# Causal attention stage: output product in two float32r parts with streamed Wo, maxima gathered by ScalarE, cosine product kept in PSUM

## The reference

```python
q = (xn @ Wq).reshape(b, n, h, dh).transpose(0, 2, 1, 3)      # 16 heads of 128
kv = xn @ Wkv
k, v = (kv[..., :dh], kv[..., dh:])                            # one key and value for all heads
q = q * cos + _rotate_half(q) * sin
k = k * cos + _rotate_half(k) * sin
q = q * scale
sim = jnp.einsum('bhid,bjd->bhij', q, k)
sim = jnp.where(causal, neg, sim)
sim = sim - jax.lax.stop_gradient(jnp.max(sim, axis=-1, keepdims=True))
attn = jax.nn.softmax(sim, axis=-1)
out = jnp.einsum('bhij,bjd->bhid', attn, v)
out = out.transpose(0, 2, 1, 3).reshape(b, n, h * dh)
return out @ Wo
```

## Time and profile before

| | us |
|---|---|
| median of 3 runs | 1264.64 (1263.53 to 1266.14) |
| profiled execution | 1257.16 |
| its span, first to last instruction | 1255.4 |
| mean granted TensorE clock in it | 0.949 of 2.4 GHz |
| attention stage in it | from 0 to about 628 |
| an ordinary step of it | 8.62 |
| a group of 8 steps | 74.5 |

### The profile page before, as it was taken

One profiled execution on the slowest core, in us unless ns is written; L12 is line 12 of the kernel. 1 busy time (PEld: TensorE's weight loads), 2 busy tenths in 40 slices (PEclk: granted clock), 3 DMA queues, 4 the chain that ended last, 5 costly groups with the idle time before them and its releaser, 6 DMA issues. The chain is left out here.

```text
span 1255.4 us, 24966 instructions
## 1 busy us (share of the span) xinstructions
PE 1071.3 (85%) x9348; PEld 728.1 (58%) x9348; DVE 889.3 (71%) x1727; ACT 565.6 (45%) x928; POOL 529.9 (42%) x464
## 2 busy tenths in 40 slices
PE   5799999999999999999855789898989963777775
PEld 5577677776777677676422566565666631333332
DVE  7977777777777777768633566767666644888884
ACT  5443333333333333335421466666656542455553
POOL 3644434343343433433324224343434344566653
PEclk9899999999999999999975899999999985899998
DMA  9220000000000000002206666667665310000000
GB/s 351 99 68 25 1 1 1 1 1 0 0 0 0 1 0 0 0 0 70 92 27 147 156 153 170 150 163 164 164 150 128 74 27 32 18 17 25 25 26 26
DMA packets 41903, 80.19 MB, mean 64 GB/s; under 512 B 9424, under 2 KB 23248, under 8 KB 38736
## 3 DMA queue, kind: packets, MB, share of 16 engines
q1 hardware_dynamic: 41136, 78.54, 23.1%
q10 hardware_dynamic: 672, 0.40, 0.1%
HBM read 61.74 MB, written 16.78 MB: 63 GB/s over the span
## 5 line engine op out<-in xcount | busy, mean ns | idle before, releaser
L356 PE MATMUL Yb<-a_Wo,a_oN 128*128 128x512 f32 x512 | 230.8, 594 | 0.0
L1210 DVE TENSOR_REDUCE mx<-Sm 128x4 f32<-128x768 f32 x128 | 122.4, 956 | 89.8 <-PE Sm L950 89.2
L543 POOL TENSOR_TENSOR a_ql<-a_rot,a_qh 128x512 fp32r<-128x512 f32 x64 | 83.9, 1315 | 176.3 <-ACT a_qh L440 176.3
L1048 ACT ACTIVATE x_ex<-Se 128x768 f32<-128x768 f32 x128 | 103.1, 805 | 119.2 <-PE Se L950 119.1
L356 PEld LDWEIGHTS Yb<-a_Wo,a_oN 128*128 128x128 f32 x512 | 97.0, 191 | 98.2 <-issue 92.9
L432 ACT ACTIVATE Lb<-Lb 128x512 f32<-128x512 f32 x64 | 37.2, 582 | 255.7 <-PE Ob L346 255.7
L277 PE MATMUL Qb<-a_xTh,WqH 128*128 128x256 f32 x512 | 146.8, 287 | 4.0 <-DVE a_vl L721 4.0
L278 PE MATMUL Qb<-a_xTl,WqH 128*128 128x256 f32 x512 | 145.5, 284 | 0.0
L279 PE MATMUL Qb<-a_xTh,WqL 128*128 128x256 f32 x512 | 145.4, 284 | 0.0
L557 POOL TENSOR_TENSOR a_pr<-a_pr_plain,a_ph 128x512 fp32r<-128x512 f32 x64 | 83.4, 1304 | 115.6 <-ACT a_ph L427 115.6
L277 PEld LDWEIGHTS Qb<-a_xTh,WqH 128*128 128x128 f32 x512 | 98.7, 193 | 8.0 <-DVE a_vl L721 3.8
(11 more groups left out here) (192 smaller groups left out, 2507.4 us busy)
## 6 DMA issues: line engine op xcount, KB each, us to landing
K<-k_parts SPq DMA_DIRECT2D x32, 256.0 KB, 4.7
q_parts<-x_qp SPq DMA_DIRECT2D x16, 384.0 KB, 3.0
Q<-q_parts SPq DMA_DIRECT2D x16, 384.0 KB, 5.7
k_parts<-x_kp SPq DMA_DIRECT2D x16, 384.0 KB, 7.3
a_w_stage<-in_gateT SPq DMA_DIRECT2D x8, 704.0 KB, 4.1
x_w_stage<-in_gateT SPq DMA_DIRECT2D x8, 704.0 KB, 5.0
WqL_plain<-in_Wq SPq DMA_DIRECT2D x4, 1024.0 KB, 11.4
a_Wo<-in_Wo SPq DMA_DIRECT2D x4, 1024.0 KB, 14.9
```

The source lines that it names most:

```text
L356: mm = pe.matmul(Yb[s % 2][:, :], oN[:, s % 2, i * P:(i + 1) * P], Wo[:, HG * u + i, :], start=(i == 0), stop=(i == HG - 1))
L543: pool.tensor_tensor(rot_dst(False, True, par, r), rbuf(par, r)[:, 0:rot_width(r)], rot_dst(True, False, par, r).bitcast(F32), ALU.subtrac ...
L1048: act.activation(ex[:, (PAIRS * b + p) % RING, 4 * hf * WIN:4 * (hf + 1) * WIN].rearrange("p (j c) -> p j c", j=2), Se[:, :, 0:2 * WIN], A ...
L1210: dve.tensor_reduce(mx[:, half, at:at + 4].rearrange("p (j a) -> p j a", j=2), Sm[:, :, 0:2 * WIN].rearrange("p j (a c) -> p j a c", a=2), ...
```

## The change

The output product is made from float32r parts: ScalarE writes the high part oH of the normalised output, GpSimd the low part oL, and out_projection runs twelve matmuls instead of four float32 ones. Wo gets a high and a low part; both for all heads don't fit in SBUF, so there are two slots, each for a quarter u. In group 0 ScalarE (out_weights_high) and GpSimd (out_weights_low, four instructions of 128 × 512 for each quarter) make them, SyncE stores each pair to DRAM (keep, 2 MB) and loads the third and fourth quarter when the slot has been read; from group 1 on GpSimd issues two 1 MB loads for a slot at the start of each even step (out_weights_again).

The maxima's four copies on VectorE become three on ScalarE, behind the exponentials (maxima_gathered); VectorE joins them after add_to_x (maxima_joined). The rotation makes the sine products first, then the cosine product in place in the PSUM bank, and the sum reads that bank; the banks are freed by rot_ready. The values' high part now waits for rot_ready too. The diff, cut to these parts:

```diff
--- before.py
+++ after.py
...
-        oN = sb("oN", [P, 2, 512], F32)
+        oN, oL = two("oN", [P, 2, 512])
+        oH = sb("oH", [P, 2, 512], F32R)
...
-        Wo = sb("Wo", [P, H, D], F32)
+        WoH = [sb(f"WoH{i}", [P, HG, D], F32R) for i in range(2)]
+        WoLp, WoL = zip(*(two(f"WoL{i}", [P, HG, D]) for i in range(2)))
+        wo_parts = nc.dram_tensor("wo_parts", (U, 2, P, HG * D), F32, kind="Internal").ap()
...
-                    pe.wait_ge(q_free, free(g, USES, j))
+                    if not isinstance(g, int) or g > 0:
+                        pe.wait_ge(rot_ready, done(g - 1, ROTS, ROTS - NG + j))
...
+                if m == 1:
+                    pe.wait_ge(q_free, done(g, NG + 1, NG))
+                elif m > 1:
+                    pe.wait_ge(rot_ready, done(g, ROTS, m - 1))
...
-                pe.wait_ge(oN_ready, done(g, STEPS, s, ON0))
-                if isinstance(g, int) and g == 0 and s % NG == 0:
-                    pe.wait_ge(wo_in[u], 16)
+                pe.wait_ge(oL_ready, done(g, STEPS, s))
+                if isinstance(g, int) and g == 0:
+                    pe.wait_ge(wo_low, HG * (u + 1))
+                else:
+                    pe.wait_ge(wo_in[u % 2], (g - 1) * (32 * U // 2) + 32 * (u // 2 + 1))
 
                 pe.wait_ge(x_new, free(g, STEPS, s))
                 for i in range(HG):
-                    mm = pe.matmul(Yb[s % 2][:, :], oN[:, s % 2, i * P:(i + 1) * P], Wo[:, HG * u + i, :],
-                                   start=(i == 0), stop=(i == HG - 1))
+                    high, low = oH[:, s % 2, i * P:(i + 1) * P], oL[:, s % 2, i * P:(i + 1) * P]
+                    pe.matmul(Yb[s % 2][:, :], high, WoH[u % 2][:, i, :], start=(i == 0), stop=False)
+                    pe.matmul(Yb[s % 2][:, :], high, WoL[u % 2][:, i, :], start=False, stop=False)
+                    mm = pe.matmul(Yb[s % 2][:, :], low, WoH[u % 2][:, i, :], start=False, stop=(i == HG - 1))
...
+            def out_weights_high(u):
+                act.wait_ge(wo_raw[u % 2], 16 * (u // 2 + 1))
+                act.activation(WoH[u % 2][:, :, :], WoLp[u % 2][:, :, :], ACT.Copy).then_inc(wo_high, 1)
+
+            def outputs_high(g, s):
+                act.wait_ge(oN_ready, done(g, STEPS, s, ON0))
+                act.activation(oH[:, s % 2, :], oN[:, s % 2, :], ACT.Copy).then_inc(oH_ready, 1)
...
+            def maxima_gathered(g, s):
+
+                act.wait_ge(rmax_ready, done(g, STEPS, s))
+                for q in range(1, 4):
+                    ins = act.activation(rmax[0:32, q, :], rmax[32 * q:32 * q + 32, 0, :], ACT.Copy)
+                ins.then_inc(mparts_ready, 1)
...
+                if real(g):
+                    maxima_gathered(g, s)
...
-                    act.wait_ge(rot_parts, done(g + 1, 2 * ROTS + 1, 2))
+                    act.wait_ge(rot_ready, done(g + 1, ROTS, 0))
...
+                if first and s in (1, 2, 5, 6):
+                    out_weights_high((0, 1, 2, 3)[(1, 2, 5, 6).index(s)])
+                if real(pg):
+                    outputs_high(pg, ps)
...
+            def keep(u):
+                sp.wait_ge(wo_low, HG * (u + 1))
+                for part, src in ((0, WoH), (1, WoL)):
+                    sp.dma_start(wo_parts[u, part], src[u % 2][:, :, :].rearrange("p h n -> p (h n)").bitcast(F32)).then_inc(wo_kept[u], 16)
+
+            def slot_read(g, u):
+                sp.wait_ge(y_full, done(g, STEPS, NG * u + NG - 1, Y0))
...
-            for u in range(U):
-                out_weights(u)
-            for n in range(len(PIECES)):
+            out_weights(0)
+            out_weights(1)
+
+            keep(0)
+            summed(0)
+            keep(1)
+            slot_read(0, 0)
+            sp.wait_ge(wo_kept[0], 32)
+            out_weights(2)
+            summed(1)
+            summed(2)
+            slot_read(0, 1)
+            sp.wait_ge(wo_kept[1], 32)
+            out_weights(3)
+            summed(3)
+            keep(2)
+            summed(4)
+            keep(3)
+            for n in range(5, len(PIECES)):
...
+            def out_weights_low(u, heads):
+                for i in heads:
+                    pool.wait_ge(wo_high, u + 1)
+                    pool.tensor_tensor(WoL[u % 2][:, i, :], WoLp[u % 2][:, i, :], WoH[u % 2][:, i, :].bitcast(F32),
+                                       ALU.subtract).then_inc(wo_low, 1)
+
+            def out_weights_again(g, u):
+
+                pool.wait_ge(wo_kept[u], 32)
+                pool.wait_ge(wo_kept[(u + 2) % U], 32)
+                pool.wait_ge(y_full, done(g, STEPS, NG * u + NG - 1, Y0))
+                pool.sem_inc(slot_free, 1)
+                for part, dst in ((0, WoH), (1, WoL)):
+                    pool.dma_start(dst[u % 2][:, :, :].rearrange("p h n -> p (h n)"),
+                                   wo_parts[(u + 2) % U, part].bitcast(F32R)).then_inc(wo_in[u % 2], 16)
+
+            def outputs_low(g, s):
+                pool.wait_ge(oH_ready, done(g, STEPS, s))
+                pool.tensor_tensor(oL[:, s % 2, :], oN[:, s % 2, :], oH[:, s % 2, :].bitcast(F32), ALU.subtract).then_inc(oL_ready, 1)
...
+                wg, ws = before(g, s, 4)
+                if real(wg) and ws % NG == 0:
+                    u = ws // NG
+                    if not isinstance(wg, int) or 0 < wg < G - 1 or wg == G - 1 and u < U - 2:
+                        out_weights_again(wg, u)
...
+                if first and s in (4, STEPS - 2):
+                    out_weights_low(1 if s == 4 else 2, (2, 3))
+                if first and s == 2:
+                    out_weights_low(0, (2, 3))
                 pg, ps = before(g, s, 1)
                 if real(pg):
                     pool.wait_ge(ph_ready, done(pg, STEPS, ps))
                     pool.tensor_tensor(pl[:, :], pr[:, :], ph[:, :].bitcast(F32), ALU.subtract).then_inc(pl_ready, 1)
+                og, os = before(g, s, 2)
+                if real(og):
+                    outputs_low(og, os)
+                if first and s == STEPS - 1:
+                    out_weights_low(3, (0, 1))
...
                     query_weights_low(7)
+                    out_weights_low(0, (0, 1))
                 if first and s == 3:
+                    out_weights_low(1, (0, 1))
                     power(2, 0)
                 if first and s == 4:
                     power(2, 1)
+                if first and s == STEPS - 3:
+                    out_weights_low(2, (0, 1))
+                if first and s == STEPS - 1:
+                    out_weights_low(3, (2, 3))
...
-                def product(dst, lo, hi, to, table, signal=rot_parts):
+                def product(dst, lo, hi, to, table):
                     dve.tensor_tensor(dst[to:to + hi - lo, 0:width].rearrange("p (j c) -> p j c", c=P),
                                       bank[lo:hi, 0:width].rearrange("p (j c) -> p j c", c=P),
                                       t[table][lo:hi, None, :].to_broadcast([hi - lo, tokens, P]),
-                                      ALU.mult).then_inc(signal, 1)
-
-                product(rbuf(par, r), 0, P, 0, "cos")
+                                      ALU.mult).then_inc(rot_parts, 1)
+
                 product(turned, 0, half, half, "sinS")
-
-                product(turned, half, P, 0, "sinS", q_free if r > 0 else rot_parts)
-                dve.wait_ge(rot_parts, done(g, 2 * ROTS + 1, 2 * r + 2))
-                if r > 0:
-                    dve.wait_ge(q_free, done(g, USES, n, QF0))
-                out = rbuf(par, r)[:, 0:width]
-                dve.tensor_tensor(out, out, turned[:, 0:width], ALU.add).then_inc(rot_ready, 1)
+                product(turned, half, P, 0, "sinS")
+
+                dve.wait_ge(rot_parts, done(g, 3 * ROTS, 3 * r + 1))
+                product(bank, 0, P, 0, "cos")
+                dve.wait_ge(rot_parts, done(g, 3 * ROTS, 3 * r + 2))
+                dve.tensor_tensor(rbuf(par, r)[:, 0:width], bank[:, 0:width], turned[:, 0:width], ALU.add).then_inc(rot_ready, 1)
...
                 dve.wait_ge(s_full, done(g, STEPS, s))
-                dve.tensor_reduce(rmax[:, :], Sb[s % 2][:, :].rearrange("p (c i) -> p c i", i=32), AX.X, ALU.max,
+                dve.tensor_reduce(rmax[:, 0, :], Sb[s % 2][:, :].rearrange("p (c i) -> p c i", i=32), AX.X, ALU.max,
                                   apply_transpose=True).then_inc(rmax_ready, 1)
-                dve.wait_ge(rmax_ready, done(g, STEPS, s))
-                for q in range(4):
-                    dve.tensor_copy(mparts[:, q, :], rmax[32 * q:32 * q + 32, :]).then_inc(mparts_ready, 1)
-                dve.wait_ge(mparts_ready, done(g, 4 * STEPS, 4 * s + 3))
+
+            def maxima_joined(g, s):
+                dve.wait_ge(mparts_ready, done(g, STEPS, s))
 
                 dve.wait_ge(dg_ready, free(g, STEPS, s))
-                dve.tensor_reduce(negm[:, :], mparts[:, :, :].rearrange("p q c -> p c q"), AX.X, ALU.max,
```

(27 more changed lines are left out.)

2 lines of the change are left out of this document (removed).

## The result

The changed kernel takes 1282.24 us (median of 4 runs, 1278.94 to 1287.79) against 1265.39 for the kernel before in the same series (1263.53 to 1266.72): ratio 1.0145, 95% interval 1.0116 to 1.0175. Predicted were 1283 (1257 to 1302) and "slower". The profiled execution of after took 1283.77 us with a span of 1282.0 and a mean granted clock of 0.929; that of before 1257.16.

What follows compares the result with a forecast made beforehand. TensorE alone was taken to set the pace between groups 1 and 6. 25 − 2.5 − 15.5 + 2.9 + 7 gives +17, clock +2: 1257.16 becomes 1276, plus 7.5 for the median: 1283 us, range 1257 to 1302.

Steps and rivals of the forecast that it cites:

- Output product: Twelve float32r matmuls on TensorE at 0.232 us take 2.78 us instead of 3.44, saving 0.66 us a step.
- ordinary step: Attention step on TensorE, from first score matmul to the next: 7.96 us instead of 8.62 if nothing else binds.
- ScalarE's late high part: High part of the output ends 0.27 into the next step, exponentials due at 0.28: nothing lost; holding ordinary steps would refute.
- The four copies go from VectorE, ... worth nothing by itself: Gathering of maxima leaves VectorE, about 1.65 us a step; not the bound, except that the rotation starts at 4.0, not 4.50.
- Step 5: In each group's step 5 TensorE idles 2.45 us for the output's low part on GpSimd; the step costs +1.8 us.
- Issues on GpSimd: From group 1, load issues ahead of the probabilities' low part take 0.9 us each, losing 0.34 a time, 7 us.
- Group 0: Making Wo's parts and a late weight piece in the first group: lag 25 us after step 0 of group 1.
- 2 for the clock: Three longer TensorE waits in group 0 may each bring a stretch at 1.2 GHz: +2 us, bounds 0 and 5.
- Last group: Five steps give −1.6 us, the last three without projections +4, the tail 0.5: +2.9 us.
- Clock rival: TensorE's idle time in each step 5 brings the 1.2 GHz level, 1.5 us a time, +12: 1295 us; chance 0.13.
- It ends faster: Wo's low parts fall into GpSimd's waits, group 0's extra below about 15 us: −21, 1244 us; chance 0.12.
- the neutral case: GpSimd issues cost 0.47 us and the weight piece isn't late: +2, 1267 us, give or take 4; chance 0.20.

Runs made afterwards that it cites:

- the three together: Changed kernel with GpSimd's output low part first in step 5, SyncE's weight piece ahead of the stores, Wo's low parts spread: 1255.35 us, ratio 0.9932.

## Why the prediction was right, point by point

**Output product and ordinary step: right.** 2.76 us for 2.78, a step of 7.94 for 7.96, no wait in it. A step isn't held by ScalarE's late high part.

**"The four copies go from VectorE, ... worth nothing by itself": the reading was right and the conclusion wrong.** Alone they are worth nothing (ratio 1.0000). Beside the new output product they are worth 46 us: the same change gave GpSimd a second pass just where the copies ran. I took 0.41 for a copy from a row of a GpSimd with one pass, and never asked what the copies would cost if they stayed. The forecast didn't need it, since the copies do go; but its account of what in the change earns its keep was wrong. The Trainium skill (SBUF — State Buffer, "Who interferes with whom") says that VectorE's copies and tensor-scalar operations can, and tensor-tensor operations with two inputs in SBUF do, contend with GpSimd for a shared port pair that is an exclusive lock, so that one of the two engines stands still. The rows agree: 0.17 us for an operation of 128 x 8 beside an idle GpSimd, 1.22 and 3.44 beside a busy one, and copies of 0.166 us of which some take 1 to 4.

**Step 5: right mechanism, half a microsecond too much.** Idle 1.84 instead of 2.45: the low part was ready at 4.07 instead of 4.2, and TensorE came 0.5 later, at 2.3 instead of 1.79. With step 6 and its neighbours a group gained 2.9 for 3.1.

**Issues on GpSimd: mis-sized.** They take 0.59 and 0.54 us (0.76 for the very first) where I took 0.9:
```profile
260.05 0.59 POOL L610 DMA_DIRECT2D a_WoH<-wo_parts  x1 [2.75 <-PE Yb L368]
260.64 0.54 POOL L610 DMA_DIRECT2D a_WoL<-wo_parts  x1
```
By my own formula a loss begins at 0.79, so the 7 us were 0 there; in the loop the loads cost 2 us. The lower bound, 0.47 from ScalarE's queue, was the nearer one. The 1 us to the first byte that I had cited isn't what the engine is held for: that is the 0.59 and 0.54, and the loads landed 5.2 and 7.1 us after their issue (medians). What the loads do cost lies in the data, which I had "come in time": some 7 us in the last group, through a weight piece that is late beside one. The term's size (7, against about 9) came out near by luck.

**Group 0: right in mechanism and place, and near in size.** Lag 28.9 at group 1's start and 27.7 a step later, where the forecast had 25 and 2 for the clock. By steps 7.7 in step 2 (6.2), 14.6 in step 4 and 19.5 in step 5 (10.2, then 11.7 and 8 more), 27.7 (25). ScalarE waited 5.45 us for the weight piece (8 forecast), which landed at 100.0 (98.5). The clock was 0.77 in the window from 37 to 112 us against 0.95 in the earlier trace rows, which I had priced at 2 us. By these means some 34 of the 75 us were at the lower level instead of 7 or 8 (an estimate); how much of the 28.9 that is, no run here separates, so the 2 us are neither confirmed nor refuted. Nor are the terms additive: removed one by one they give 19.7 us, removed together 16.4.

**Last group: mis-sized.** Forecast +2.9, measured +10.1. The last three steps are as forecast: TensorE's wait there is 5.47 us instead of 4.09, the +1.4 of the prediction. The step that failed is that I looked for chains only there and not at step 5. ScalarE waits 3.63 us for a piece whose transfer runs beside a reload of Wo issued at 605.36, and the wait goes through exponentials, the probabilities' low part and the low part of the output:
```profile
605.36 0.59 POOL L610 DMA_DIRECT2D a_WoH<-wo_parts  x1 [0.21 <-issue]
...
616.54 1.48 ACT L511 ACTIVATE a_w_stage<-a_w_stage 128x1536 f32<-128x1536 f32 x1 [3.63 <-DMA a_w_stage<-in_downT]
...
621.87 0.80 PE L366 MATMUL Yb<-a_WoH,a_oH 128*128 128x512 f32 x1 [7.98 <-POOL a_oN L615]
```
Without the reloads no piece is late and the group costs 3.2, close to the forecast. With the low part first, the piece is as late (3.82), but the wait ahead of the output product is 1.1 and the one behind it, for the probabilities, 2.8. The two remedies reach the same loss: without the late piece, or with the order that doesn't hand it on, the group costs 6 to 7 us less. So the order in step 5 was worth 19 us and not 8: it also passed each delay of the exponentials on to TensorE, at both ends.

**Clock rival: the mechanism is real, its condition was wrong.** I gave it 0.13 for "each step 5". It is not each: none, one, three, five or six of six, with the same idle time, and 1.5 us a time was the right price (1.57). The four executions of the changed kernel spread over 9 us; whether they differ by this isn't known, since only one of them has a profile.

**The other rivals.** "It ends faster" asked for less than 15 us in group 0. The changed kernel has 27.9; where the work was ordered so that it has 11.5 or 9.4, the time is indeed under that of before (1255 and 1250, for 1244 forecast), but some 16 of the 30 us that the former gains on the changed kernel's profiled execution lie outside group 0, where the order in step 5 is changed too. Of the neutral case half came true: the issues cost GpSimd next to nothing, but the piece was late.

**The sum.** 19 was forecast for the profiled execution, 26.6 measured. The terms differ so (rounded): issues −7, the rest of the loop +2, last group +7, group 0 +1, next stages +5, which the forecast had at nothing. Their code is unchanged and TensorE's clock goes through other levels at their start (0.53 and 0.62 in the first two stretches of 10 us, 0.56 and 0.75 before); that this makes the 5 us isn't shown. The 7.5 us added for the median were too much by 9: that of after lies 1.5 below its profiled execution. So it is luck that 1283 hits 1282 so closely, where two errors of 8 and 9 us cancel; the sign, and the places in group 0 that made it, are not.

## What to carry to other kernels

Price an engine's spare time by who stands still beside whom: work taken from VectorE was worth nothing until GpSimd got a second pass, and then 46 us. A mean of many short operations can hide it; look at the median and the longest. When an in-order engine serves two consumers, look at each step whose order on the consuming engine is different (here step 5): put first what is wanted first, or every delay upstream is handed on. Where the time spreads over more than a remedy is worth, judge the remedy by the lag of its own stage: two that changed the time by 3.4 and 1.6 us, within the noise, took over 6 us each from group 0, and the three together 16. And ask of each new transfer which other one is in flight beside it: the reloads cost the engine that issued them almost nothing, and the last group 7 us.

## What the runs showed of the hardware

- One idle time of TensorE of 1.84 us is followed by a stretch near 1.2 GHz in some cases and in others not, in one and the same program (1, 3 or 5 of 6), and costs 1.57 us when it is; 2.84 us were followed by it in five of six cases, at 1.6 to 2.7 us. What decides stays open.
- VectorE's operations of 128 x 8 took 0.17 us beside an idle GpSimd and 1.2 to 3.4 beside a busy one; copies of 32 x 16 took 0.166 at the median and up to 1.54 and 4.04, on average 0.37 and 0.61; two row operations of 128 x 512 took 1.95 and 5.57.
- GpSimd spends 0.54 to 0.59 us on the issue of a 1 MB load (0.76 for its first); ScalarE spends 0.22 us on a copy of 32 x 16 across partitions.
